# Holding a scatter of token rows to two transfers under way

## The chip, the cores and the metric

The kernel runs on one core of a Trainium2 chip, in one launch. The metric is the device time of that core in microseconds. The engines are PE (TensorE), DVE (VectorE), ACT (ScalarE), POOL (GpSimd) and SP (SyncE); SP computes nothing here and issues DMAs. Each engine runs its own instruction stream, and the streams meet only at semaphores.

## The reference, cut to what matters

Two layers on a residual stream x of 4 x 512 tokens of 256 floats. Each layer is a gated cross-attention and then a gated feed-forward part. The last feed-forward part, where the change lies, is a mixture of 8 experts with 2 chosen per token, beside a shared expert that every token passes:

```python
def _L1_ffn_ref(x, gate_w, experts_gate_up, experts_down, shared_gate_w, shared_up_w, shared_down_w, shared_expert_gate_w):
    x_flat = x.reshape(Bx * Tx, H)                       # 2048 tokens x 256
    scores = jax.nn.softmax(x_flat @ gate_w.T, axis=-1)
    _, topk_ids = jax.lax.top_k(scores, 2)
    w = scores * jax.nn.one_hot(topk_ids, E, dtype=x.dtype).sum(axis=1)
    gu = jnp.einsum('nh,eih->nei', x_flat, experts_gate_up)
    h = jax.nn.silu(gu[..., :I]) * gu[..., I:]           # I = 352
    out = jnp.einsum('neh,ne->nh', jnp.einsum('nei,ehi->neh', h, experts_down), w)
    shared = jax.nn.silu(x_flat @ shared_gate_w.T) * (x_flat @ shared_up_w.T) @ shared_down_w.T
    return out + jax.nn.sigmoid(x_flat @ shared_expert_gate_w.T) * shared
...
x = x + tanh(g_xattn[0]) * attention_0(layernorm(x), ctx)
x = x + tanh(g_ffn[0])   * routed_ffn(layernorm(x))
x = x + tanh(g_xattn[1]) * attention_1(layernorm(x), ctx)
x = x + tanh(g_ffn[1])   * _L1_ffn_ref(layernorm(x), ...)
```

## The kernel before, in words

The phases follow each other: projections and attention of layer 0, its routed feed-forward part, projections and attention of layer 1, the output projection, and then `mixture_phase` (from L998), which starts at about 710 us of the span. Only this last phase is touched.

The mixture computes each expert on just the tokens that chose it. The 2048 tokens lie in SBUF as `sb.tok`, in TT = 16 tiles of 128 rows, a row having 256 floats and 4 words more that hold its number. Every token has two choices (c = 0 and 1), so 4096 rows are sorted by expert. DVE works out for each (token, choice) a slot number (`slots`, L1381 to L1414). POOL then writes the rows to a scratch in HBM, `slots_in`, with one indirect DMA for each tile and choice: 128 rows of 1040 bytes, each to the slot that `m.slot` names (L1120 to L1129). That makes 2 x 16 = 32 indirect DMAs. Between the two halves POOL rewrites the number in each row of `sb.tok` (iota, L1123), and for that it waits for all transfers of the first half (L1122), which read it. All 32 count up one semaphore, `scattered`, by 16 each as they land.

SP waits until all 32 have landed (L1067) and then loads the slots in tiles of 128 (`xg`, L1078). For each of 39 slot tiles PE transposes the rows (`turn_x`, L1209), multiplies by the gate and up weights of the tile's expert (`up`, L1218), transposes the product (L1228) and multiplies by the down weights (L1236). ACT applies silu and copies, DVE multiplies and copies. POOL copies the rows' numbers (`keep_id`, L1135) and scatters the results to `slots_out` (`scatter_y`, L1140).

While the scatter runs, PE, ACT and DVE work on the shared expert, which is cut into 2 halves by 4 batches of 512 tokens, called blocks. Five blocks come before the expert tiles (`early_blocks`, L1039) and three after. A block has three up tiles (L1169, 8 matmuls each), for each of which ACT makes silu from PSUM into `g` (L1295) and DVE multiplies it by the other half of PSUM into `h` (L1422). Then come four down tiles (L1183, 6 matmuls each), each added to `x` by DVE (L1429). PE may start an up tile only when DVE has multiplied the last but one, and a down tile only when DVE has added the last but one. The order of the work on each engine is written out by hand. PE's first transpose of a slot tile comes after the fifth block and waits for its last add (L1250), for the first slot tile's load (L1206) and for the expert weights.

Of the kernel before, what the change touches and what calls it, by code (L numbers as in the profile page):

```python
# [26 lines left out]
TT = N // P  # L27
# [970 lines left out]
def mixture_phase(nc, sem, sb, m, args, scr, zeroed, out):  # L998
# [11 lines left out]
    UP = B * len(IC)  # L1010
    logits_kept, exp_done = sem("logits_kept"), sem("scores_exp")
    shared_gate, hot_ready, ranks_done = sem("shared_gate"), sem("hot_ready"), sem("ranks_done")
    slots_ready, scattered = sem("slots_ready"), sem("scattered")
    chain = sem("route_chain")
    half_loaded = m.half_loaded
    experts_loaded = sem("experts_loaded")
# [29 lines left out]
    def tiles(eng, body):  # L1046


        body(0, True, False)
        with eng.Fori(1, ST // 4 - 1) as it:  # L1050
            body(it, False, False)
        body(ST // 4 - 1, False, True)

    def step_tiles(last):

        return LAST_STEP if last else 4

    with nc.Block() as block:
        @block.sync
        def _(sp):  # L1060
            for e in range(E):
                sp.dma_start(m.gu[:, e, :, :], args["gate_up"][e].rearrange("(c p) f -> p c f", p=P)
                             ).then_inc(experts_loaded, 16)
            for i, (a, n) in enumerate(IC):
                sp.dma_start(m.dn[0:n, :, i, :], args["down"][0:E, a:a + n, :].rearrange("e p f -> p e f")
                             ).then_inc(experts_loaded, 16)
            sp.wait_ge(scattered, 16 * 2 * TT)  # L1067

            def slot_tile(buf, it, u):

                return buf.rearrange("(i u p) d -> i u p d", u=4, p=P)[
                    bass.ds(it, 1), u, :, :].rearrange("i p d -> (i p) d")

            def body(it, first, last):
                for u in range(step_tiles(last)):
                    sp.wait_ge(x_turned, it * 4 + (u + 1))
                    sp.wait_ge(id_kept, it * 4 + (u + 1))
                    sp.dma_start(m.xg[:, u, :], slot_tile(scr.xs, it, u)).then_inc(xg_loaded[u], 16)  # L1078
            tiles(sp, body)
            for u in range(4):  # L1080

                sp.wait_ge(y_stored[u], 16 * (ST // 4 - (0 if u < LAST_STEP else 1)))
            for b in range(B):
                for c in range(2):
                    sp.dma_start(m.yg[c][:, QT * b:QT * (b + 1), 0:D],
                                 scr.ys[c * N + b * S:c * N + (b + 1) * S, :].rearrange("(t p) d -> p t d", p=P)
                                 ).then_inc(y_loaded[b], 16)
            for b in range(B):
                sp.wait_ge(y_added, 2 * QT * (b + 1))
                sp.wait_ge(x_added, TT + QT * (b + 1))  # L1090
                sp.dma_start(out[b].rearrange("(t p) d -> p t d", p=P), sb.x[:, b * QT:(b + 1) * QT, :]
                             ).then_inc(out_done, 16)
            sp.wait_ge(out_done, 16 * B)

        @block.gpsimd
        def _(pool):

            nc.gpsimd.memset(m.tri[:, 0, :], 1.0).then_inc(padded, 1)
            pool.wait_ge(padded, 1)
            nc.gpsimd.memset(m.tri[:, 1, :], 1.0).then_inc(padded, 1)  # L1100
            pool.wait_ge(padded, 2)
            nc.gpsimd.affine_select(out=m.tri[:, 0, :], in_=m.tri[:, 0, :], compare_op=ALU.is_gt, fill=0.0,
                                    base=0, pattern=[[1, P]], channel_multiplier=-1).then_inc(padded, 1)
            pool.wait_ge(padded, 3)
            nc.gpsimd.iota(m.count_i[:, :], pattern=[[1, ST]], base=0, channel_multiplier=0).then_inc(padded, 1)
            pool.wait_ge(padded, 4)
            nc.gpsimd.tensor_copy(m.count[:, :], m.count_i[:, :]).then_inc(padded, 1)
            pool.wait_ge(padded, 5)

            nc.gpsimd.memset(m.hs[:, :, I1:len(IC) * P], 0.0).then_inc(padded, 1)  # L1110
            pool.nop().then_inc(x_turned, 4)
            pool.nop().then_inc(id_kept, 4)
            nc.gpsimd.memset(sb.tok[:, :, D:DW], 0.0).then_inc(rows_named, 1)
            pool.wait_ge(rows_named, 1)
            nc.gpsimd.iota(sb.tok[:, :, D].bitcast(I32), pattern=[[P, TT]], base=0,
                           channel_multiplier=1).then_inc(rows_named, 1)
            pool.wait_ge(rows_named, 2)
            pool.wait_ge(zeroed, 16 * (H // HG + 1))
            pool.wait_ge(slots_ready, 1)
            for c in range(2):  # L1120
                if c == 1:
                    pool.wait_ge(scattered, 16 * TT)  # L1122
                    nc.gpsimd.iota(sb.tok[:, :, D].bitcast(I32), pattern=[[P, TT]], base=N,  # L1123
                                   channel_multiplier=1).then_inc(rows_named, 1)
                    pool.wait_ge(rows_named, 3)
                for t in range(TT):
                    pool.indirect_dma_start(  # L1127
                        out=scr.xs, out_offset=bass.IndirectOffsetOnAxis(ap=m.slot[:, c, t:t + 1], axis=0),
                        in_=sb.tok[:, t, :], in_offset=None).then_inc(scattered, 16)  # L1129

            def keep_id(it, u):
                pool.wait_ge(xg_loaded[u], (it + 1) * 16)
                if it:
                    pool.wait_ge(y_stored[u], it * 16)
                nc.gpsimd.tensor_copy(m.id[:, u:u + 1], m.xg[:, u, D:D + 1].bitcast(U32)).then_inc(id_kept, 1)  # L1135

            def scatter_y(it, u):
                pool.wait_ge(id_kept, it * 4 + (u + 1 + 4))
                pool.wait_ge(y_kept, it * 4 + (u + 1 + 2))
                pool.indirect_dma_start(  # L1140
                    out=scr.ys, out_offset=bass.IndirectOffsetOnAxis(ap=m.id[:, u:u + 1], axis=0),
                    in_=m.y[:, u, :], in_offset=None).then_inc(y_stored[u], 16)

            def body(it, first, last):
                for u in range(step_tiles(last)):
                    keep_id(it, u)
                    if u:
                        scatter_y(it, u - 1)
                    elif not first:
                        scatter_y(it - 1, 3)  # L1150
                if last:
                    scatter_y(it, LAST_STEP - 1)
            for it in range(ST // 4):
                body(it, it == 0, it == ST // 4 - 1)
# [339 lines left out]
def build(nc, a, out):  # L1494
    ctx = ExitStack()
    with ctx:
# [74 lines left out]
        for layer in range(2):  # L1571
# [24 lines left out]
            with ExitStack() as fm:  # L1596
# [51 lines left out]
                else:  # L1648
# [45 lines left out]
                    m.logits_done = sem("logits_done")  # L1694
                    output_phase(nc, sem, sb, aw, "o1_", lambda sp, s: load_gate(sp, m, a, s), None, m)
                    mixture_phase(nc, sem, sb, m, a, scratch, zeroed, out)


# [77 lines left out]
```

## Time and profile before

| | us |
|---|---|
| median of 3 runs | 1037.14 |
| the runs | 1032.03, 1037.14, 1039.59 |
| profiled execution, its own time | 1031.81 |
| its span | 1029.7 |
| busy in the span: PE / DVE / ACT / POOL | 961.3 / 578.7 / 481.8 / 582.6 |
| mean granted TensorE clock | 0.965 |

All rows come from this one profiled execution, with times counted from the start of its span. An engine's idle time is given in square brackets with what ended it; "issue" means that the profile shows nothing the engine waited for, and "remote" that the semaphore was raised but the trace doesn't say by which instruction. The row of an indirect DMA on POOL is the issuing of it; its data moves later.

### The profile page before, as it was taken

The numbers are of one execution on the slowest core, as the hardware profiler recorded it, in microseconds if no ns is written. First come the engines' busy times: TensorE is split into PE (matmuls) and PEld (weight loads), VectorE is DVE, ScalarE is ACT, GpSimd is POOL, SyncE is SP. The second block draws the span as 40 slices with busy tenths as digits, with TensorE's granted clock in tenths as the row PEclk, the third lists the DMA queues.
The fourth block names the chain that finished last, engine by engine and source line by source line (L and its number), as shares of the span: only waits on it lengthen the run. The fifth ranks groups of instructions, "written<-read, shape, count | busy, mean of one in ns | idle before, by whom it ended". The sixth has DMA issues, their size and how long they took to land. (4 is left out here: it accounts for less than half of the span.)

```text
span 1029.7 us, 21406 instructions
## 1 busy us (share of the span) xinstructions
PE 961.3 (93%) x7727; PEld 548.6 (53%) x7728; DVE 578.7 (56%) x1698; ACT 481.8 (47%) x660; POOL 582.6 (57%) x617
## 2 busy tenths in 40 slices
PE   6989999999987998969999999989987999999997
PEld 3544444444473544634444444476543677777654
DVE  4878888888570116768888888664421222222236
ACT  2448777877742112437877877732110123222210
POOL 3469999999637502479999999730065022222300
PEclk9989999999997998989999999996998999999999
DMA  9573827283002332472433334023622022222152
GB/s 298 195 224 63 223 55 219 53 227 63 2 22 82 127 129 76 137 171 58 102 60 88 89 63 114 2 85 142 195 89 99 22 63 66 62 66 62 37 168 82
DMA packets 86612, 107.56 MB, mean 104 GB/s; under 512 B 9664, under 2 KB 68632, under 8 KB 86520
## 3 DMA queue, kind: packets, MB, share of 16 engines
q1 hardware_dynamic: 75816, 85.08, 30.0%
q0 software_dynamic: 4848, 14.70, 4.3%
q10 hardware_dynamic: 5856, 6.56, 2.0%
q8 instruction: 58, 0.95, 0.4%
q14 instruction: 34, 0.28, 0.1%
HBM read 76.92 MB, written 29.38 MB: 103 GB/s over the span
## 5 line engine op out<-in xcount | busy, mean ns | idle before, releaser
L605 ACT ACTIVATE pT<-ps 128x1024 f32<-128x1024 f32 x256 | 248.6, 1023 | 95.0 <-PE ps L477 94.7
L647 POOL TENSOR_TENSOR xT<-nmax,xT 128x512 f32<-128x512 f32 x192 | 195.7, 1042 | 18.8 <-DVE nmax L545 18.4
L647 POOL TENSOR_TENSOR s<-nmax,s 128x512 f32<-128x512 f32 x192 | 196.6, 1041 | 14.1 <-DVE nmax L545 10.0
L545 DVE CUSTOM_DVE_ANT_0 s<-ps,bias 128x512 f32<-128x512 f32 x256 | 166.1, 689 | 42.6 <-PE ps L464 41.3
L545 DVE CUSTOM_DVE_ANT_0 xT<-ps,bias 128x512 f32<-128x512 f32 x256 | 166.6, 689 | 40.0 <-PE ps L464 32.2
L464 PE MATMUL ps<-ks,qs 97*128 97x512 bf16 (+1 forms) x512 | 160.2, 393 | 11.8 <-DVE nmax L545 4.8
L492 PE MATMUL ps<-pT,vq 128*32 128x512 f32 x1024 | 135.1, 604 | 2.4
L1140 POOL DMA_INDIRECT slots_out<-y,id x39 | 38.3, 983 | 137.6 <-DVE y L1463 134.3
L464 PEld LDWEIGHTS ps<-ks,qs 97*128 97x128 bf16 (+1 forms) x512 | 30.4, 97 | 129.9 <-DVE nmax L545 63.8
L1218 PE MATMUL ps<-gu,xgT 128*128 x312 | 98.8, 460 | 0.7 <-ACT xgT L1301 0.7
L1169 PE MATMUL ps<-xT,sgu 128*128 128x512 f32 (+1 forms) x192 | 89.4, 622 | 9.1 <-issue 7.0
L477 PEld LDWEIGHTS ps<-ident,xT 64*128 64x128 f32 x2048 | 70.1, 141 | 28.6 <-issue 28.3
L477 PEld LDWEIGHTS ps<-ident,s 64*128 64x128 f32 x2048 | 70.0, 141 | 20.7 <-issue 19.4
L1457 DVE TENSOR_TENSOR hs<-gs,ps 128x352 f32<-128x352 f32 x39 | 20.4, 522 | 107.8 <-ACT gs L1306 107.8
L477 PE MATMUL ps<-ident,s 64*128 64x64 f32 x2048 | 78.8, 228 | 1.0 <-issue 1.0
L477 PE MATMUL ps<-ident,xT 64*128 64x64 f32 x2048 | 79.0, 228 | 0.0
L1218 PEld LDWEIGHTS ps<-gu,xgT 128*128 128x128 f32 x312 | 56.2, 190 | 25.7 <-issue 0.9
L186 POOL TENSOR_TENSOR parts<-rest,parts 128x512 bf16<-128x512 f32 x32 | 38.2, 1194 | 55.0 <-DVE parts L307 55.0
L1169 PEld LDWEIGHTS ps<-xT,sgu 128*128 128x128 f32 (+1 forms) x192 | 36.2, 191 | 58.6 <-issue 54.5
L1295 ACT ACTIVATE g<-ps 128x512 f32<-128x512 f32 (+1 forms) x24 | 14.3, 597 | 106.9 <-PE ps L1169 70.8
L1236 PE MATMUL ps<-dn,hT 128*128 (+1 forms) x234 | 57.1, 380 | 0.7 <-ACT hT L1311 0.7
L1127 POOL DMA_INDIRECT slots_in<-tok,slot x32 | 31.0, 968 | 45.3 <-DVE tile_expert L1414 35.9
(164 smaller groups left out, 1226.1 us busy)
## 6 DMA issues: line engine op xcount, KB each, us to landing
bias<-in_bias SPq DMA_DIRECT2D x16, 1024.0 KB, 5.8
qk_scratch<-parts SPq DMA_DIRECT2D x64, 128.0 KB
qs<-qk_scratch SPq DMA_DIRECT2D x32, 192.0 KB, 3.4
ks<-qk_scratch SPq DMA_DIRECT2D x32, 192.0 KB, 3.9
gu<-in_gate_up SPq DMA_DIRECT2D x8, 704.0 KB, 9.6
slots_in<-zeros POOLq DMA_DIRECT2D x4, 1280.0 KB, 7.1
xg<-slots_in SPq DMA_DIRECT2D x39, 130.0 KB, 2.0
qk_scratch<-parts ACTq DMA_DIRECT2D x32, 128.0 KB
```

The source lines that it names most:

```text
L186: nc.gpsimd.tensor_tensor(sb.parts[:, n % PARTS, 2, :], sb.rest[:, n % 4, :], sb.parts[:, n % PARTS, 1, :], ALU.subtract).then_inc(low_don ...
L464: nc.tensor.matmul(sb.ps[:, ring_bank(place), :], at.qs[0:K, b % 2, j, qt * P:(qt + 1) * P], at.ks[0:K, b % 2, j, :], start=True, stop=Tru ...
L477: last = nc.tensor.transpose(sb.ps[:, 2 + kt // 2 * 2 + r, col:col + HP], at.s[m % 4][rows, qt, kt * P:(kt + 1) * P], sb.ident[rows, rows])
L492: last = nc.tensor.matmul(sb.ps[VW * j:VW * (j + 1), 6, :], at.vq[:, b % 2, kt, j, :], pair[:, kt % 2, :, :, :], start=(kt == 0), stop=(kt ...
L545: nc.vector.tensor_tensor_reduce(at.s[m % 4][:, qt, :], sb.ps[:, ring_bank(tile_place[u - 1 + hg * 64]), :], at.bias[:, j if per_head_bias ...
L605: nc.scalar.activation(at.pT[:, slot(m // HG, m % HG), 2 * half:2 * half + 2, :], sb.ps[:, 2 + 2 * half:4 + 2 * half, :], ACT.Exp).then_in ...
L647: nc.gpsimd.tensor_tensor(s, at.nmax[:, m % 4, qt:qt + 1].to_broadcast([P, S]), s, ALU.subtract).then_inc(pool_less_max, 1)
L1127: pool.indirect_dma_start(out=scr.xs, out_offset=bass.IndirectOffsetOnAxis(ap=m.slot[:, c, t:t + 1], axis=0), in_=sb.tok[:, t, :], in_offs ...
L1140: pool.indirect_dma_start(out=scr.ys, out_offset=bass.IndirectOffsetOnAxis(ap=m.id[:, u:u + 1], axis=0), in_=m.y[:, u, :], in_offset=None) ...
L1169: last = nc.tensor.matmul(sb.ps[0:n, 2 * (k % 2) + g, :], m.sgu[:, half, c, g * I1 + a:g * I1 + a + n], sb.xT[:, c, b * S:(b + 1) * S], st ...
L1218: last = nc.tensor.matmul(sb.ps[:, 2 * (u % 2) + g, 0:I1], m.xgT[:, u % 2, c, :], m.gu[:, bass.ds(e, 1), c, g * I1:(g + 1) * I1].rearrange ...
L1236: last = nc.tensor.matmul(sb.ps[:, 6 + u % 2, 0:D], m.hT[0:n, u % 2, i, :], m.dn[0:n, bass.ds(e, 1), i, :].rearrange("p e f -> p (e f)"), ...
```

## The change

`scattered` becomes two semaphores, used by even and odd tiles. In each half, POOL issues tiles 0 and 1 freely. From tile 2 on it waits, before it issues tile t, until tile t - 2 has landed. The two places that waited for all transfers, POOL's between the halves and SP's before its loads, now wait for both semaphores. The transfers, their order and their data stay the same.

```diff
-    slots_ready, scattered = sem("slots_ready"), sem("scattered")
+    slots_ready, scattered = sem("slots_ready"), [sem(f"scattered{i}") for i in range(2)]
...
-            sp.wait_ge(scattered, 16 * 2 * TT)
+            for i in range(2):
+                sp.wait_ge(scattered[i], 16 * TT)
...
             for c in range(2):
                 if c == 1:
-                    pool.wait_ge(scattered, 16 * TT)
+                    for i in range(2):
+                        pool.wait_ge(scattered[i], 16 * TT // 2)
                     nc.gpsimd.iota(sb.tok[:, :, D].bitcast(I32), pattern=[[P, TT]], base=N,
                                    channel_multiplier=1).then_inc(rows_named, 1)
                     pool.wait_ge(rows_named, 3)
                 for t in range(TT):
+                    if t >= 2:
+                        pool.wait_ge(scattered[t % 2], 16 * (c * TT // 2 + t // 2))
                     pool.indirect_dma_start(
                         out=scr.xs, out_offset=bass.IndirectOffsetOnAxis(ap=m.slot[:, c, t:t + 1], axis=0),
-                        in_=sb.tok[:, t, :], in_offset=None).then_inc(scattered, 16)
+                        in_=sb.tok[:, t, :], in_offset=None).then_inc(scattered[t % 2], 16)
```

## Rows read from the trace of the kernel before

**Rows 1.** The page: busy time of PE, and the group of the scatter's issues.
```profile
PE 961.3 (93%) x7727; PEld 548.6 (53%) x7728; DVE 578.7 (56%) x1698; ACT 481.8 (47%) x660; POOL 582.6 (57%) x617
...
L1127 POOL DMA_INDIRECT slots_in<-tok,slot x32 | 31.0, 968 | 45.3 <-DVE tile_expert L1414 35.9
```

**Rows 2.** Chain that ended last, 745 to 815: start, duration, what.
```profile
747.52 3.67 PE ps L1169 x8
751.19 5.19 PE ps L1183 x24
756.38 10.30 PE ps L1169 x24
766.68 2.60 PE ps L1183 x12
769.28 3.27 issue
772.55 4.30 PE ps L1183 x12
776.85 7.27 PE ps L1169 x16
784.12 7.00 issue
791.12 5.39 PE ps L1169 x8
796.51 10.40 PE ps L1183 x48
...
806.93 0.49 DVE x L1429
807.43 0.35 issue
807.78 0.43 PE ps L1209 x2
```

**Rows 3.** Timeline of POOL, 747 to 791: start, duration, what [idle before].
```profile
747.79 1.08 POOL L1127 DMA_INDIRECT slots_in<-tok,slot  x1 [35.87 <-DVE tile_expert L1414]
...
766.96 0.96 POOL L1127 DMA_INDIRECT slots_in<-tok,slot  x1 [0.30 <-issue]
769.52 0.15 POOL L1123 IOTA tok<- 128x16 int32 x1 [1.59 <-DMA slots_in<-tok,slot]
769.95 0.98 POOL L1127 DMA_INDIRECT slots_in<-tok,slot  x1 [0.28 <-issue]
...
787.70 0.96 POOL L1127 DMA_INDIRECT slots_in<-tok,slot  x1 [0.30 <-issue]
788.97 0.96 POOL L1127 DMA_INDIRECT slots_in<-tok,slot  x1 [0.30 <-issue]
```

**Rows 4.** Timelines of SP and POOL at the first load of slots.
```profile
791.53 20.74 SPq L1078 DMA_DIRECT2D xg<-slots_in  x6
...
793.62 0.19 POOL L1135 COPY id<-xg 128x1 uint32<-128x1 uint32 x1 [3.69 <-DMA xg<-slots_in]
```

**Rows 5.** Timeline of ACT, 763 to 791.
```profile
763.46 0.60 ACT L1295 ACTIVATE g<-ps 128x512 f32<-128x512 f32 x1 [3.01 <-PE ps L1169]
770.54 0.59 ACT L1295 ACTIVATE g<-ps 96x512 f32<-96x512 f32 x1 [6.49 <-remote]
789.75 0.60 ACT L1295 ACTIVATE g<-ps 128x512 f32<-128x512 f32 x1 [18.61 <-remote]
```

**Rows 6.** Timeline of DVE: two adds during the scatter, two after it.
```profile
777.04 0.48 DVE L1429 SCALAR_TENSOR_TENSOR x<-ps,w,x 128x256 f32<-128x256 f32 x1 [3.10 <-PE ps L1183]
781.98 0.48 DVE L1429 SCALAR_TENSOR_TENSOR x<-ps,w,x 128x256 f32<-128x256 f32 x1 [4.45 <-remote]
...
799.14 0.48 DVE L1429 SCALAR_TENSOR_TENSOR x<-ps,w,x 128x256 f32<-128x256 f32 x1 [0.82 <-PE ps L1183]
800.44 0.48 DVE L1429 SCALAR_TENSOR_TENSOR x<-ps,w,x 128x256 f32<-128x256 f32 x1 [0.81 <-PE ps L1183]
```

**Rows 7.** Timelines of POOL and DVE: an indirect DMA that waits, in the expert loop.
```profile
817.11 0.42 DVE L1463 COPY y<-ps 128x256 f32<-128x256 f32 x1 [0.50 <-PE ps L1236]
...
818.31 0.98 POOL L1140 DMA_INDIRECT slots_out<-y,id  x1 [23.95 <-DVE y L1463]
```

**Rows 8.** Windows: busy time of each engine, granted clock, DMA share, GB/s.
```profile
748.00:769.00 21.00, 21.00 (x68) 12.14 (x66) 4.40 (x8) 1.79 (x3) 15.35 (x16) 1.00 0.29 102
...
773.00:784.00 11.00, 11.00 (x28) 5.76 (x26) 1.45 (x3) 0.00 (x0) 8.26 (x10) 0.84 0.28 101
784.00:791.00 7.00, 0.12 (x1) 0.00 (x0) 0.62 (x1) 0.60 (x1) 4.71 (x5) 0.77 0.32 114
791.00:796.00 5.00, 4.88 (x8) 1.82 (x9) 0.76 (x2) 0.60 (x1) 0.38 (x2) 0.64 0.38 107
```

## The prediction

> **What bounds the kernel now.** I began with the page. PE is busy for 93% of the span, and the indirect DMAs that put token rows into expert slots are 32 instructions on POOL with 31.0 us of issuing between them [rows 1]. An edit there can matter only if something on the way to the end waits for POOL or for these transfers, so I went to the chain of waits around the scatter. From 747.52 to 806.91 the chain is PE's shared-expert products, with two holes, 3.27 us at 769.28 and 7.00 us at 784.12. It then passes through DVE's last add and PE's first transpose of a slot tile at 807.78 [rows 2]. The scatter is not in it.
>
> How far off is it? POOL issues the first transfer at 747.79 and the last at 788.97 [rows 3]. SP, which waits for all 32, issues the first load of slots at 791.53, and POOL's copy, which waits for that load, starts at 793.62 [rows 4]. So slots are at hand 2.09 us after SP's issue. PE has no use for them before DVE's add ends at 807.43. **The slack is 807.43 - 793.62 = 13.8 us.**
>
> The two holes lie inside the scatter's stretch, so I looked at what fills them. At 769.28 PE needs a product from DVE, which needs ACT's activation at 770.54. ACT had sat idle 6.49 us before that. At 784.12 the same happens: ACT's activation starts at 789.75 after 18.61 us of idle time, released by something the trace calls remote [rows 5]. Yet the eight matmuls it needs are the first half of the piece at 776.85, and by the spacing in that piece (16 in 7.27 us) they ended at about 780.5. ACT therefore started some 9 us after its input was written. DVE shows the same at 781.98, where an add starts 5.1 us after the matmuls for it ended at 776.85 [rows 2, 6]. I read this as news from PE that reaches ACT and DVE late while the scatter runs. After 791 it is prompt again: DVE's adds follow each other at 1.30 us, each released by PE's own row [rows 6].
>
> **The change part by part.**
>
> *The hold.* From the third transfer of each half on, POOL waits for the last but one: 14 waits a half, 28 in all. Issues are 1.27 us apart (0.96 of issuing and 0.30 between), so the last but one was issued 2.54 us before. How long does landing take? The trace has two places where an engine waits for a last transfer alone. POOL's iota starts at 769.52 after an issue at 766.96, and SP's load starts at 791.53 after an issue at 788.97. Both are 2.56 us, with the release of the waiting engine inside [rows 3, 4]. So before the change a transfer had already landed, or was about to, when the next but one was issued: **there are about two under way without the hold.** A waiting issue comes 2.56 - 2.54 = 0.02 us later than now. Each of the two chains of alternating transfers meets 7 waits a half, and the cost is 14 x 0.02 = 0.3 us over the scatter. This is the lower bound too, since a wait can't bring an issue forward.
>
> The upper bound comes from another row. In the expert loop an indirect DMA that has to wait for DVE's copy starts at 818.31, and that copy ended at 817.11 + 0.42 = 817.53. That is 0.78 us from release to start [rows 7]. If it all comes on top of the 2.56, a pair takes 3.34 us in place of 2.54, and 14 pairs take 11.2 us more. I take 0.3 us. The iota's wait is on the same transfers, and the indirect DMA behind it starts 0.27 us after the iota's end (769.52 + 0.15 to 769.95), so a wait just before such an issue need not cost 0.78. Both ends stay in the range.
>
> A sentence on the skill, which the sum does not use: the Trainium skill (DMA: Bandwidth & Descriptors, "Anatomy of one DMA") puts a DMA issued by GpSimd at about 2.0 us plus its bytes over 436 GB/s. For 128 rows of 1040 bytes I estimate 2.31 us by it, less than the 2.54 us between an issue and the next but one, so by that page no wait would ever hold and the hold would cost 0. The trace's 2.56 us, with a release in it, neither confirms nor excludes this.
>
> *What is behind POOL's waits.* Queued behind them on POOL are the iota, the second half, and the copies of slot numbers. SP waits for all 32 landings. PE waits for SP's loads. With 0.3 us added, slots are ready at 793.9, with 11.2 us at 804.8, and PE wants them at 807.43. **Both ends are hidden**, the second by only 2.6 us. If the cover shrank by the whole 13.8 us, the delay would show in full.
>
> *The iota's wait and SP's wait* become two waits each. Both counters stand at their values when the last transfer lands, so one of the pair passes at once. POOL's small waits have no row of their own here. I put them between nothing and the 0.30 us that lie between two issues [rows 3], take nothing for both, and they too lie under the slack. No transfer, byte or compute instruction is removed, and nothing moves on PE, DVE or ACT.
>
> **The sum** is 0 us at the end of the program. The profiled execution took 1031.81 us with a span of 1029.7, which is 5.3 us under the median of the runs shown (1037.14). The three runs lie 7.6 us apart, so I put the forecast on their median: **1037 us**. A change of 1% is about 10 us, and that is what this kernel's measurement can tell from none.
>
> **Rivals.**
>
> *First rival: the late news from PE goes away.* All late starts lie while the scatter's traffic flows. If that traffic causes them, and if a slightly slower or more even stream no longer does, the holes close. The gain is 3.27 + 7.00 = 10.3 us. There is also PE's clock. The granted clock is 0.84 in 773 to 784 and 0.64 in 791 to 796, against 1.00 in 748 to 769 [rows 8]. This follows each hole. Like with like, 12 down matmuls take 4.30 us against 2.60, 16 up matmuls 7.27 against 6.87 (two thirds of 10.30), and 8 take 5.39 against 3.67, in sum 3.8 us [rows 2]. All this makes 14.1 us, of which the slots' own readiness leaves 13.8 - 0.3 = 13.5, hence 1037.1 - 13.5 = 1023.6 us. If the hold costs its upper bound, the stream is slowest and the late news likeliest to end, but slots come at 804.8 and only 2.6 us can be had. Half a cure lies between. Against this rival: at my price of a wait the traffic thins by 1%, and two were under way anyway. For it: ACT and DVE are prompt again once the traffic stops. Chance 0.22, with a little over half of it beyond 1%, as a cure with cheap waits is the only way to that size.
>
> A related rule of the skill speaks for the forecast and against this rival. The Trainium skill (NOTIFIC — the notification-queue block, "Overflow: three behaviours, one of which stalls the engine") says that the block which writes trace records can push back on the engines that feed it. If the late news is that, a hold on the scatter would leave it much as it is, and the time would stay at the forecast. No row here can show whether it is.
>
> *Second rival, slower: late news that lasts as long as the scatter does.* ACT's late activation starts at 789.75, 0.78 us after the last issue at 788.97 [rows 3, 5]. If PE's news is held until POOL has issued its last transfer, then whatever lengthens the scatter lengthens the hole at 784.12 one for one, and the slack of 13.8 us is no cover. At 0.3 us that is nothing. At 0.78 us a wait in place of the iota row's 0.27 it is 14 x (0.51 + 0.02) = 7.4 us, or 1044.5 us, and at the upper bound 11.2 us, or 1048.3. It decides once a wait costs 0.7 us over the present spacing of a pair, where 14 of them pass 10 us. Against it: the iota row, and that ACT's first late start, at 770.54, came 3.6 us after the first half's last issue at 766.96, so the two are not tied that closely. Chance 0.18, half of it beyond 1%.
>
> *The forecast*, no visible change, keeps 0.60. It contains the case in which the change does not do what it says, because the hold is already nearly met.
>
> **How the numbers follow.** Faster by over 1%: 0.14, from the first rival. Slower by over 1%: 0.09, from the second. Within 1%: 0.77. The range runs from 1025 us, nearly all of the cure, to 1046 us, the second rival with its dearer waits but short of the upper bound. The runs' own spread of 7.6 us lies inside it.
>
> **What the changed kernel's profile would show.** The 32 scatter issues: 1.27 to 1.29 us apart if the waits are nearly met, 1.5 to 1.7 if the 0.78 is real. POOL's idle time before them would be put down to the transfers, or remain issue. The first load of slots at 2.6 us after the last issue. The chain should still run through PE from 747 to 807 with holes of about 10 us in sum, and PE's first transpose should come after DVE's add, not after a load. If the holes are gone and the transpose waits for the load, the first rival holds. If scatter and holes have both grown, the second does. The forecast would be wrong in its first step if the issues were more than 1.35 us apart, and in its last if the late starts on ACT changed by several microseconds either way.

## The result, and the profile after

The changed kernel takes **1028.6 us** (median of 18 runs, 1024.1 to 1033.51) against 1038.68 us (18 runs). The ratio is **0.9908, with a 95% interval of 0.9887 to 0.9928**. That is 0.9% faster, just inside the 1% that the prediction called no change, though the interval reaches past it. The profiled execution has a span of 1026.8 us.

The chain that ended last, from the changed kernel's trace (start, duration, what; its shortest pieces are left out). It answers to [rows 2]:

```profile
788.09 2.28 DMA slots_in<-tok,slot
790.37 0.84 issue
791.20 0.96 POOL slots_in L1131
792.16 0.30 issue
792.47 2.54 DMA slots_in<-tok,slot
795.29 2.29 DMA slots_in<-tok,slot
797.58 0.43 issue
798.00 2.50 DMA slots_in<-tok,slot
800.56 2.06 DMA xg<-slots_in
802.87 0.68 PE ps L1213 x2
803.57 0.39 ACT xgT L1305
804.09 4.53 PE ps L1222 x8
```

PE is gone from the chain in the scatter's stretch. The end now hangs on the transfers themselves: POOL waits, issues, waits. ACT's timeline answers to [rows 5]. Every activation is released by PE's own row, after 2.84 us of idle time within a block, and "remote" has vanished:

```profile
770.03 0.59 ACT L1299 ACTIVATE g<-ps 96x512 f32<-96x512 f32 x1 [2.84 <-PE ps L1173]
778.66 0.60 ACT L1299 ACTIVATE g<-ps 128x512 f32<-128x512 f32 x1 [8.03 <-PE ps L1173]
782.09 0.60 ACT L1299 ACTIVATE g<-ps 128x512 f32<-128x512 f32 x1 [2.84 <-PE ps L1173]
785.52 0.59 ACT L1299 ACTIVATE g<-ps 96x512 f32<-96x512 f32 x1 [2.84 <-PE ps L1173]
```

POOL's timeline, answering to [rows 3]: first, second and third issue, two in the middle, the iota and the last:

```profile
751.11 1.08 POOL L1131 DMA_INDIRECT slots_in<-tok,slot  x1 [35.86 <-DVE tile_expert L1418]
752.50 0.98 POOL L1131 DMA_INDIRECT slots_in<-tok,slot  x1 [0.30 <-issue]
754.10 0.96 POOL L1131 DMA_INDIRECT slots_in<-tok,slot  x1 [0.62 <-DMA slots_in<-tok,slot]
...
758.14 0.96 POOL L1131 DMA_INDIRECT slots_in<-tok,slot  x1 [0.34 <-DMA slots_in<-tok,slot]
761.23 0.96 POOL L1131 DMA_INDIRECT slots_in<-tok,slot  x1 [2.13 <-DMA slots_in<-tok,slot]
...
776.32 0.15 POOL L1125 IOTA tok<- 128x16 int32 x1 [1.61 <-DMA slots_in<-tok,slot]
...
798.00 0.96 POOL L1131 DMA_INDIRECT slots_in<-tok,slot  x1 [0.44 <-DMA slots_in<-tok,slot]
```

The waits do hold: 23 issues waited for a transfer, 12.4 us in all. The last issue comes 46.9 us after the first, where it was 41.2. And PE now waits for the slots:

```profile
802.87 0.66 PE L1213 MATMUL ps<-ident,xg 128*128 128x128 f32 x2 [7.00 <-DMA xg<-slots_in]
```

The granted clock, answering to [rows 8], is 1.00 in every stretch of the scatter in which PE works, up to 796:

```profile
773.00:784.00 11.00, 11.00 (x32) 5.58 (x31) 2.46 (x5) 1.19 (x2) 6.57 (x9) 1.00 0.20 73
784.00:791.00 7.00, 7.00 (x31) 5.48 (x30) 2.40 (x5) 0.59 (x1) 4.62 (x5) 1.00 0.28 101
```

Behind PE's new wait, from 802 to 812, it is 0.70.

**The account of the two traces.** The first issue stands at 751.11 against 747.79, a difference that earlier phases bring. From there to PE's first transpose it is 51.8 us against 60.0, so 8.2 us less. From there to the end it is 2.0 us more, nearly all of it because eight matmuls after PE's long wait take 4.53 us instead of 2.64. Together +3.3 - 8.2 + 2.0 = -2.9, by which the spans differ. The medians differ by 10.1 us. The execution profiled before was faster than all 18 runs, and its stage was not a long one: in the traces of experiments 1, 2 and 4 below, which have late starts too, PE's first transpose comes 56.8, 63.3 and 63.5 us after the first issue. With the 63.4 us of experiments 2 and 4, whose own times (1040.58 and 1039.47 us) lie near the median before, I estimate 63.4 - 51.8 - 2.0 = 9.6 us for the change.

### The profile page after: what moved, and what is told of

The parts are those of the page before. It is cut to its first block and busy times, and to the rows that moved or that the text cites. A ratio compares the mean times of both kernels' runs of the same rounds, so it can differ in the third digit from the quotient of the medians.

```text
span 1026.8 us, 21408 instructions
## 1 busy us (share of the span) xinstructions
PE 964.6 (94%) x7727; PEld 550.8 (54%) x7728; DVE 578.6 (56%) x1698; ACT 481.9 (47%) x660; POOL 582.7 (57%) x617
## 5 line engine op out<-in xcount | busy, mean ns | idle before, releaser
L464 PE MATMUL ps<-ks,qs 97*128 97x512 bf16 (+1 forms) x512 | 163.3, 400 | 9.1 <-POOL xT L647 3.3
L1173 PE MATMUL ps<-xT,sgu 128*128 128x512 f32 (+1 forms) x192 | 86.9, 609 | 2.2 <-DVE h L1426 1.4
```

What stands on the lines that cost most here:

```text
L464: nc.tensor.matmul(sb.ps[:, ring_bank(place), :], at.qs[0:K, b % 2, j, qt * P:(qt + 1) * P], at.ks[0:K, b % 2, j, :], start=True, stop=Tru ...
L1173: last = nc.tensor.matmul(sb.ps[0:n, 2 * (k % 2) + g, :], m.sgu[:, half, c, g * I1 + a:g * I1 + a + n], sb.xT[:, c, b * S:(b + 1) * S], st ...
```

## The experiments

The first eight ran on one chip, in two groups with their own runs of the kernel before (1036.92 us, 31 runs, and 1035.21 us, 12 runs). The last four ran on another chip, and that turned out to matter. Which chip the comparison above ran on is not known. Its time before (1038.68 us) and its late starts are like the first chip's. "Late" is said of an engine that starts several microseconds after PE ended the matmuls it needs.

**1. Four under way.**

```diff
-                    if t >= 2:
-                        pool.wait_ge(scattered[t % 2], 16 * (c * TT // 2 + t // 2))
+                    if t >= 4:
+                        pool.wait_ge(scattered[t % 4], 16 * (c * TT // 4 + t // 4))
```

> The hold is loosened: four semaphores, tile t waits until tile t-4 has landed, 12 waits a half instead of 14. Landing takes 2.56 us and four issues take 5.08 us, so the waits should be met long before they are asked. Theory A (only a hold that binds helps, by thinning the stream): issues stay 1.27 us apart, PE's news is late again, and the time is that of the kernel before, 1038 us within 4. Theory B (the waits by themselves, or the alternating semaphores, are what helps): the late starts on ACT are gone, 1029 us within 3.

1034.0 us, ratio 0.9975 (0.9949 to 1.0001). The spacing is 1.27 us and the late starts are back. ACT's timeline:

```profile
772.55 0.59 ACT L1299 ACTIVATE g<-ps 96x512 f32<-96x512 f32 x1 [6.49 <-remote]
786.87 0.60 ACT L1299 ACTIVATE g<-ps 128x512 f32<-128x512 f32 x1 [13.72 <-remote]
```

PE's holes are 3.2, 3.8 and 0.6 us. The waits and semaphores by themselves are not the cure (theory B falls), if perhaps a small part of it.

**2. A one-column memset between issues.** `nc.gpsimd.memset(m.pad[:, c * TT + t:c * TT + t + 1], 0.0)` before each issue but the first of a half, in the kernel before.

> The kernel before with no wait on a landing, but a small memset of one column on POOL between two scatter issues, which should put them about 1.40 us apart (0.96 of issuing, 0.15 of memset, 0.28 up to the next). The change's own spacing was 1.43 us on average. Theory A (the density of the stream makes PE's news late): late starts gone, 1029 us within 3. Rival C (what helps is that POOL stops when landings are late, a feedback that a fixed pace lacks): the holes return in part or whole, 1033 to 1039 us.

1038.4 us, ratio 1.0020 (0.9986 to 1.0053). It tested nothing on pace. The memset took 0.12 us inside the 0.30 us gap, and the spacing stayed 1.27 us. The holes were there, 5.4, 2.0 and 4.6 us.

**3. The hold in the first half only.** `if t >= 2 and c == 0:`

> The change with its waits in the first half of the scatter only; the second half is issued freely, 1.27 us apart. Theory A: PE's news is prompt in the first half and late in the second, as it was in the kernel before at 776 to 793; the hole before the last up tile comes back, and the time lies between the two, 1031 to 1037 us. If a delay must build up over both halves (a backlog that starts in the first), the second half stays clean: about 1027 us, since the scatter is then shorter by some 2 us than in the change.

1029.78 us, ratio 0.9934 (0.9905 to 0.9963). The first half is clean. In the second the news is late only from about 786 on, 12 us after its first issue at 774.35, and PE's holes are 4.0 us in sum. PE's timeline:

```profile
782.34 5.36 PE L1187 MATMUL ps<-sdn,h 128*128 128x256 f32 x24
788.41 1.53 PE L1187 MATMUL ps<-sdn,h 128*128 128x256 f32 x6 [0.72 <-issue]
791.88 2.93 PE L1187 MATMUL ps<-sdn,h 128*128 128x256 f32 x6 [1.93 <-issue]
796.12 5.49 PE L1187 MATMUL ps<-sdn,h 128*128 128x256 f32 x12 [1.32 <-issue]
```

So a free half does less harm behind a held one. That fits something that builds up, but does not show it.

**4. Rows of 64 floats instead of 260**, scattered freely to a scratch that nothing reads. The experts then compute on zero rows, and the output lacks their part. Not shown are the scratch's declaration and the changed place from which results are read.

```diff
-                        out=scr.xs, out_offset=bass.IndirectOffsetOnAxis(ap=m.slot[:, c, t:t + 1], axis=0),
-                        in_=sb.tok[:, t, :], in_offset=None).then_inc(scattered, 16)
+                        out=scr.short, out_offset=bass.IndirectOffsetOnAxis(ap=m.slot[:, c, t:t + 1], axis=0),
+                        in_=sb.tok[:, t, 0:64], in_offset=None).then_inc(scattered, 16)
...
```

> The kernel before with free issues, but each scattered row is 64 floats instead of 260, to a scratch that nothing reads, so the experts compute on zero rows and the output lacks them. As many issues at the same spacing, a quarter of the bytes. Theory D (bytes on the way to HBM make PE's news late): late starts gone; PE free of holes, and first transposes after about 793 us of the span, so 1024 to 1029 us. Theory E (issuing itself, or the number of pieces and landings, does it): late starts as before, 1038 us within 4.

1038.94 us, ratio 1.0021 (0.9990 to 1.0052). With a quarter of the bytes the late starts stay, so it is not bandwidth (theory D falls). ACT's timeline:

```profile
774.75 0.59 ACT L1295 ACTIVATE g<-ps 96x512 f32<-96x512 f32 x1 [5.12 <-remote]
797.43 1.09 ACT L1295 ACTIVATE g<-ps 128x512 f32<-128x512 f32 x2 [22.09 <-remote]
```

**5. A real pace without a hold.** The kernel before with `nc.gpsimd.memset(m.pad[:, :], 0.0)` of 128 x 256 between issues. Each memset but the first waits for the memset before it, which has long ended.

> The one-column memset of the pace experiment ran inside the 0.30 us gap, so the spacing stayed 1.27 us and nothing was tested. This one puts a memset of 128 x 256 between two issues (0.31 us by the same form elsewhere in the profile), with no wait on any landing. Spacing about 1.45 us, last issue 46 to 48 us after the first as in the change. Theory A (density of the stream): PE's news is prompt, no holes, 1029 us within 3. Rival C (the stop that answers a late landing is what helps): holes as before, 1036 to 1040 us.

**1027.3 us, ratio 0.9929 (0.9905 to 0.9952).** The spacing is 1.46 us, where the hold's was 1.45 on average within the halves. There is no hole in PE's shared-expert work, and POOL waits for no landing inside a half. POOL's and PE's timelines:

```profile
750.13 0.97 POOL L1133 DMA_INDIRECT slots_in<-tok,slot  x1 [0.17 <-issue]
751.10 0.33 POOL L1132 MEMSET pad<- 128x256 f32 x1
751.59 0.97 POOL L1133 DMA_INDIRECT slots_in<-tok,slot  x1 [0.17 <-issue]
...
798.86 0.66 PE L1215 MATMUL ps<-ident,xg 128*128 128x128 f32 x2 [7.04 <-DMA xg<-slots_in]
```

So the gain needs no stop that answers a late landing (rival C falls); a thinner stream is enough. This run can't tell it from a bound on transfers under way, since 2.92 us between an issue and the next but one also leave about two. The next one can.

**6. One pause in each half.** `if t == 8: pool.wait_ge(scattered, 16 * (c * TT + t))` in the kernel before.

> The kernel before with one pause in each half: before its ninth transfer POOL waits until the first eight have landed. All else is issued freely at 1.27 us. It costs about 1.7 us a pause, 3.4 in all. In the runs so far the news was never late in the first 14 us of a free stream, neither in the kernel before nor in the second half that was left free behind a held first half. If a backlog has to build up and drains in a pause, four stretches of 10 us never let it get far: holes gone or under 2 us, 1027 to 1031 us. If density over the whole scatter decides (1.38 us on average here), part of the holes stays: 1032 to 1037 us.

1024.74 us (4 runs), ratio 0.9901 (0.9867 to 0.9934). There is no late start, though 28 of the 31 steps between issues are the free 1.26 to 1.38 us. So neither a bound of two nor a slow pace throughout is needed. (The expectation says that news was never late in the first 14 us of a free stream. In experiment 3 it was, about 12 us in; the stretches here last 10.) POOL's timeline at the pause:

```profile
759.29 0.96 POOL L1129 DMA_INDIRECT slots_in<-tok,slot  x1 [0.30 <-issue]
761.99 0.95 POOL L1129 DMA_INDIRECT slots_in<-tok,slot  x1 [1.74 <-DMA slots_in<-tok,slot]
```

Slots come sooner than with the hold: PE's first transpose is 48.8 us after the first issue, against 51.8.

**7. A sixth shared-expert block early.** `EARLY = 2` in the changed kernel.

> The change with one more block of the shared expert ahead of the expert tiles (EARLY = 2). In the changed kernel PE idles from 795.9 until slots come at 802.9 and then runs its first tiles at half clock, some 7 + 1.9 us. A block is 15.5 us of PE work, so it fills the gap, and the transposes start about 61 us after the first issue. The end is 15.5 us shorter on PE but DVE's adds of expert results are less covered there. Expected 1024 us, 1021 to 1028; if DVE's tail takes all of it, 1029.

1026.01 us (5 runs), ratio 0.9916 (0.9890 to 0.9943). The gap before the first transpose is filled. Of the 8.9 us that wait and slow clock had cost, the traces keep a gain of 2.8 from the first issue to the end. The rest is given back at the end, where DVE's adds of expert results end the chain.

**8. The same, with DVE's expert adds first.**

```diff
                 shared_prod(*late_blocks[n])
-                shared_add(*late_blocks[n - 1])
                 if n == 1:
                     for b in range(EARLY):
                         expert_add(b)
+                shared_add(*late_blocks[n - 1])
```

> As the run before, with DVE's adds of expert results for the first two batches put ahead of its adds of the first late block. They then run while PE does down products. Expected 1 to 3 us less than the run before, 1022 us; not better if DVE was not what the tail waited for.

**1018.94 us (5 runs), ratio 0.9841 (0.9807 to 0.9874)**, the fastest on this chip. From the first transpose to the end it is 209.0 us, against 211.7 in the run before. PE no longer waits for the slots, here as in the run before:

```profile
801.23 10.55 PE L1187 MATMUL ps<-sdn,h 128*128 128x256 f32 x48
812.67 0.41 PE L1213 MATMUL ps<-ident,xg 128*128 128x128 f32 x2 [0.89 <-DVE x L1433]
```

**9 to 12, on another chip.** There the kernel before takes **1020.6 us** (25 runs, 1016.9 to 1026.11).

**9.** The pace of experiment 5 with a memset of 128 x 128.

> The real pace again with a memset of 128 x 128 (0.20 us by its row) between issues, no wait on a landing: spacing about 1.35 us, where 1.27 has the holes and 1.47 has none. If the limit lies just above 1.27 (a backlog fills slowly, by what exceeds the drain), PE's news is prompt or nearly so and the scatter is 4 us shorter than with 1.47: 1024 to 1027 us. If the limit lies between 1.35 and 1.47, part of the holes is back: 1029 to 1034 us.

1024.46 us, ratio 1.0033 (1.0010 to 1.0056), slower. The spacing is 1.35 us, and PE waits for slots and then runs slowly (the row has seven matmuls; all eight take 4.5 us):

```profile
800.87 0.66 PE L1215 MATMUL ps<-ident,xg 128*128 128x128 f32 x2 [3.72 <-DMA xg<-slots_in]
802.09 4.22 PE L1224 MATMUL ps<-gu,xgT 128*128 x7 [0.56 <-ACT xgT L1307]
```

It gives no threshold, since this chip shows no late news to cure.

**10.** The kernel of experiment 8 once more, with the hold.

> The best version so far once more for one look, as a control for the two beside it: the hold, six early blocks, DVE's expert adds first. 1019 us within 4, no holes in PE during the scatter.

1023.03 us in a single run. From the first transpose to the end it is again 209.0 us.

**11.** The kernel of experiment 8 without the hold (`EARLY = 2` and the order of adds, in the kernel before).

> That version without the hold: six early blocks, DVE's expert adds first, the scatter issued freely as in the kernel before. PE's early work always ends after the slots are in, so it gains what the later block and the new order of adds are worth, but PE's news should be late again with holes of about 10 us and 3 us of slow clock after them. Expected 1030 us, 1026 to 1033. If the late news cost nothing beyond its holes and the sixth block hid them, it would be 1019 us like the version with the hold.

1021.89 us, ratio 1.0011 (0.9986 to 1.0036), **against the expectation of late news.** The scatter runs freely, and ACT follows PE at once:

```profile
785.24 0.96 POOL L1127 DMA_INDIRECT slots_in<-tok,slot  x1 [0.30 <-issue]
786.50 0.96 POOL L1127 DMA_INDIRECT slots_in<-tok,slot  x1 [0.30 <-issue]
...
779.36 0.60 ACT L1295 ACTIVATE g<-ps 128x512 f32<-128x512 f32 x1 [8.04 <-PE ps L1169]
782.79 0.60 ACT L1295 ACTIVATE g<-ps 128x512 f32<-128x512 f32 x1 [2.83 <-PE ps L1169]
786.22 0.59 ACT L1295 ACTIVATE g<-ps 96x512 f32<-96x512 f32 x1 [2.83 <-PE ps L1169]
```

PE's part of the chain of waits has no hole in it:

```profile
770.69 5.19 PE ps L1183 x24
775.88 10.30 PE ps L1169 x24
786.18 5.19 PE ps L1183 x24
791.38 10.30 PE ps L1169 x24
801.68 10.40 PE ps L1183 x48
```

**12.** Six early blocks with the single pause.

> Six early blocks and DVE's expert adds first, with the single pause in each half in place of the hold. Slots are in 3 us sooner than with the hold, but PE does not wait for them any more. Expected 1019 us, 1017 to 1022, the same as with the hold; 1023 and more if the pause lets some late news through.

1022.39 us, ratio 1.0014 (0.9990 to 1.0038). No late news, no gain. The slots were expected 3 us sooner than with the hold, but were in at the same time (50.8 us after the first issue against 50.7 in experiment 10), because SP's first load started 4.6 us after the last issue, where it is 2.56 in [rows 3] and [rows 4]. That costs nothing, as PE starts on the slots at 61.2 us.

## Why the prediction was right, and where it was not

**The time** lies in the range (1025 to 1046) and within 1%, but 8 us under the forecast, and not by the forecast's mechanism. That it fits is luck: the forecast was no effect, and what happened is the first rival, to which I gave 0.22. The holes went, and a cure that the dearer waits cut short ended at 0.9%.

**Two under way without the hold: right.** Loosened to four, the hold never binds and the spacing stays 1.27 us, with 7.5 us of holes (experiment 1).

**The price of a wait: mis-sized.** I took 2.56 us from an issue to the next but one and 0.3 us over the scatter, with 11.2 as the other end. In the trace after, such pairs are mostly 2.7 to 3.0 us and the scatter is 5.7 us longer: 47 us of issues for 41. Two overlapping pairs took 4.4 us (3.09 us from 758.14 to 761.23). The two rows I measured from were both the last transfer of a run, with no other behind it. That is only part of the matter: in the later traces POOL's iota started 2.50 to 2.73 us after such a last issue (all but experiment 4), and POOL's next issue 2.69 to 2.81 after it at the pauses of experiments 6 and 12. So my 2.56 was a value from the lower half of a spread. What makes the rest of the price is not shown.

**The slack of 13.8 us hides it: wrong once the holes go.** The cover was made of the holes and of slow clock. Without them PE is done 44.8 us after the first issue, slots are ready after 51.5, and 7.0 us of wait plus 1.9 us of slow clock remain. The rival's working covers this only for cheap waits. With 5.7 us for them it gives 13.8 - 5.7 = 8.1 us for the stage, and 8.2 was measured, but it leaves out the 1.9 us of clock after PE's new wait.

**Late news: the reading was right, the odds were not.** One detail was misread: at 769.28 PE waited for DVE's add at 772.01, which stood behind the late product in DVE's order, and only at 784.12 for a product itself. The forecast of no effect failed here: it took it that nothing moves on PE, DVE or ACT. I argued that traffic thinned by 1% could hardly help. The waits thinned it by 12%. A pace of 1.46 us does the same with no hold, and so does one pause in eight, which points to a backlog that fills in a dense stretch and drains in a gap. No run shows such a backlog itself. A quarter of the bytes doesn't help, so it goes with the number of transfers, their pieces or their issuing. Which of these, no run here tells apart.

**The second rival** (late news to the end of a longer scatter) did not occur. (Its 14 waits at 0.7 us make 9.8 us, not quite the 10 it speaks of; nothing rests on it.)

**What stays open.** On the second chip a free scatter makes no late news, and the kernel before is 15 to 18 us faster there. The two chips are otherwise much alike: from the first transpose to the end the kernel of experiments 8 and 10 takes 209.0 us on both. The kernel of experiment 8 reaches 1018.94 us on the first chip, about what the kernel before takes on the second, so the gains here may be no more than a cure for what is amiss on the first. The kernel before has no trace from the second chip. That its news is prompt there rests on experiment 11, whose scatter is the same, and on its time.

The recording differs between the chips too. Each of the 32 transfers lands with 16 semaphore records, 512 in all. The four traces with long holes (the kernel before, experiments 1, 2 and 4) hold 120 to 130 of them, those of experiments 3 and 6 hold 267 and 205, of the changed kernel and experiments 7 and 8 326, 310 and 319, of the real pace 447, and the four of the second chip 511 or 512. So records were lost wherever news was late, but also in experiments 5 to 8 and the changed kernel, where it was not. The Trainium skill (NOTIFIC — the notification-queue block, "Overflow: three behaviours, one of which stalls the engine") says that the block which writes records can stall the engine that feeds it, but lists that and losing the record as different behaviours. The losses here are therefore no sign of a stall by that page. That recording causes the late news is neither shown nor excluded: no run here was made without recording.

The changed kernel wasn't run on the second chip. Experiment 9's ratio makes the 1.35 us spacing cost 3.4 us there, and with the hold slots come 3.3 us later still (first transpose 51.8 us after the first issue, against 48.5). From these I estimate that the change would be some 7 us slower than the kernel before.

**The best version** is experiment 8 on the first chip. On the second chip the same choices (experiments 11 and 12) are no faster than the kernel before.

## What to carry to other kernels

An engine that starts several microseconds after its input was written is waiting for news, not for work: compare its start with the end of the matmuls it needs before trusting a slack. A cover that consists of such holes is no cover for what a change adds. And where a change's gain rests on a delay between engines, time it on a second chip before keeping it.

## What the runs showed of the hardware

While POOL issued indirect DMAs 1.27 us apart, semaphores raised by PE reached ACT and DVE up to 9 us late on one chip, first some 12 to 19 us into a dense stretch, and not at all late at 1.46 us, with a pause after eight, or, at the same 1.27 us, on another chip (experiment 11). DVE's news to PE was prompt: in the kernel before, the product below ended at 791.07 and let PE go on at 791.12 [rows 2]. In the changed kernel an indirect DMA that waited for the last but one mostly started 2.7 to 3.0 us after that one's issue. After an idle stretch of 3.7 to 7.0 us (experiments 5, 6, 9 and the changed kernel), PE's first eight up matmuls of a slot tile took 4.3 to 4.8 us in place of 2.6.

```profile
790.38 0.69 DVE L1422 TENSOR_TENSOR h<-g,ps 128x512 f32<-128x512 f32 x1 [7.92 <-issue]
```
